# One input of two-input VectorE instructions moved from SBUF to PSUM in a four-block graph network

## What is computed

```
x = layernorm(x + L0(x))   # s, v = x @ w;  w0..w3 = silu(edge_attr_8 @ fc1) @ fc2 ;  tensor products of
                           # s[src], v[src] with edge_attr_4 and w0..w3;  segment_sum over dst;  @ w_lin2
x = layernorm(x + L1(x))   # four GCN layers (widths 128, 256, 256, 256 gathered), segment_sum over dst
x = layernorm(x + L2(x))   # mean of x[dst] over each src;  relu(x @ W_self.T + mean @ W_neigh.T + b)
x = layernorm(x + L3(x))   # attention of two heads: e = leaky_relu(a_src[src] + a_dst[dst]),
                           # alpha = segment_softmax(e, dst), segment_sum(xs[src] * alpha, dst), prelu
```

## Time and profile before

| | |
|---|---|
| median of 3 runs | 9904.8 us (9901.6 to 9915.3) |
| the profiled execution | 9888.5 us, span 9886.7 us |
| granted TensorE clock, mean | 0.777 |
| busy: POOL, PE, DVE, ACT | 6902, 5937, 5561, 2664 us |

### The profile page before, as it was taken

One profiled execution on the slowest core, in us unless ns is written; L12 is line 12 of the kernel. 1 busy time (PEld: TensorE's weight loads), 2 busy tenths in 40 slices (PEclk: granted clock), 3 DMA queues, 4 the chain that ended last, 5 costly groups with the idle time before them and its releaser, 6 DMA issues. The chain is left out here.

```text
span 9886.7 us, 100742 instructions
## 1 busy us (share of the span) xinstructions
PE 5937.4 (60%) x23034; PEld 4208.1 (43%) x23034; DVE 5560.9 (56%) x14363; ACT 2663.7 (27%) x8909; POOL 6902.3 (70%) x7265
## 2 busy tenths in 40 slices
PE   0676745555566665666656666555554444588785
PEld 0343433333444443444434444333343333476674
DVE  9307037777655556555565555544444333488887
ACT  0332335555322223111131111200001000366665
POOL 0678757777677765777657776577777777577775
PEclk9999986777788887888878888677765555577877
DMA  7111123333311122333323333233332111212112
GB/s 268 48 58 48 58 70 101 101 102 102 54 52 52 52 46 82 100 100 100 88 84 100 100 100 86 81 101 100 99 89 58 53 53 53 44 48 49 49 48 41
DMA packets 344415, 770.69 MB, mean 78 GB/s; under 512 B 121029, under 2 KB 175577, under 8 KB 337226
## 3 DMA queue, kind: packets, MB, share of 16 engines
q0 software_dynamic: 251328, 600.99, 23.1%
q1 hardware_dynamic: 85066, 105.97, 3.5%
q10 hardware_dynamic: 7488, 57.94, 1.5%
HBM read 616.04 MB, written 148.41 MB: 77 GB/s over the span
## 5 line engine op out<-in xcount | busy, mean ns | idle before, releaser
L566 DVE TENSOR_TENSOR acc<-acc,ps 128x256 f32 (+3 forms) x4992 | 1884.0, 377 | 2859.7 <-PE ps L903 2403.0
L903 PE MATMUL ps<-rows,hot 128*128 128x256 f32 (+2 forms) x5824 | 1645.2, 442 | 1712.3 <-issue 871.1
L741 POOL DMA_INDIRECT rows<-table_gcn,index_dst x2080 | 2082.6, 1001 | 684.9 <-issue 608.2
L903 PEld LDWEIGHTS ps<-rows,hot 128*128 128x128 f32 x5824 | 1281.7, 272 | 2152.3 <-issue 1145.9
L786 ACT ACTIVATE ut<-u,fld 128x128 f16<-128x128 f16 x1664 | 576.7, 393 | 2732.8 <-DVE u L829 2732.8
L497 POOL DMA_INDIRECT dst_rows<-pay,acc x782 | 798.7, 1021 | 529.5 <-ACT pay L481 304.6
L741 POOL DMA_INDIRECT rows<-table_gat,index_dst x832 | 913.1, 1097 | 262.6 <-issue 253.3
L741 POOL DMA_INDIRECT rows<-table_lin,index_dst x832 | 860.3, 1034 | 335.2 <-issue 241.4
L741 POOL DMA_INDIRECT rows<-table_mean,index_src x832 | 795.0, 955 | 259.0 <-issue 253.2
L718 PE MATMUL ps<-prod,hot 128*128 128x257 f32 x1664 | 637.4, 550 | 535.4 <-issue 347.5
L875 PE MATMUL ps<-prod,ut 128*128 128x416 f16 x3328 | 889.3, 399 | 0.0
(11 more groups left out here) (270 smaller groups left out, 9196.2 us busy)
## 6 DMA issues: line engine op xcount, KB each, us to landing
dst_rows<-pay ACTq DMA_DIRECT2D x52, 1088.0 KB, 31.6
fld<-dst_rows SPq DMA_DIRECT2D x104, 544.0 KB, 3.5
rows<-table_gcn,index_dst POOLq DMA_INDIRECT x2080, 2.5
table_gcn<-acc SPq DMA_DIRECT2D x15, 1024.0 KB
rows<-table_lin,index_dst POOLq DMA_INDIRECT x832
rows<-table_mean,index_src POOLq DMA_INDIRECT x832, 2.5
rows<-table_gat,index_dst POOLq DMA_INDIRECT x832
dst_rows<-pay,acc POOLq DMA_INDIRECT x782, 2.3
```

The costliest lines, as they stand in the source:

```text
L566: c.nc.vector.tensor_tensor(to, to, product, ALU.add).then_inc(c.added.sem, 1)
L741: pool.indirect_dma_start(to(q, j), None, table, bass.IndirectOffsetOnAxis(ap=c.idx[k][:, t:t + 1], axis=0)).then_inc(c.gathered[q % per]. ...
L903: pe.matmul(c.ps[:, j % ahead, 0:used], c.hot[:, r % 2, j, :], row_of(c, s, r, j, used), start=True, stop=True).then_inc(c.mm.sem, 1)
```

## The change

- In `sort_dve` the scan's operand of ones becomes one PSUM column, repeated.
- In all passes the one-hot's `c.iota` comes from a copy in PSUM (bank 3, in the attention bank 7), which ScalarE writes once a pass.
- In `messages` ScalarE writes the scaled vectors to PSUM banks 4 to 7, in one copy and not two; it waits for the same half of the group before. Products use three banks and not eight.
- In `aggregate` products use three banks, not four or eight.
- In `attend` ScalarE takes the exponential twice, first into PSUM (read by line 1969 as its second input), then into the weights' own columns (`m.kept`); products use two banks, not three.

Cut to its core:

```diff
@@ sort_dve
+    ones = c.ps[:, banks[1], 0:1]
+    st(dve.memset(ones, 1.0)).wait()
...
-            st(dve.tensor_tensor_scan(runs[i], s.one_row[:, :], masks[i], base[:, bass.ds(b * 2 + i, 1)],
+            st(dve.tensor_tensor_scan(runs[i], ones.broadcast_to([P, TC]), masks[i], base[:, bass.ds(b * 2 + i, 1)],
@@ helpers
+PLACES = 3
+def lay_places(c, act, bank=PLACES):
+    act.activation(c.ps[:, bank, 0:P], c.iota[:, :], ACT.Copy).then_inc(c.places_laid.sem, 1)
+def wait_places(c, dve):
+    dve.wait_ge(c.places_laid.sem, c.places_laid.n + 1)
 def one_hot(c, h, places):
-    c.nc.vector.tensor_tensor(c.hot[:, h, :, :], c.iota[:, :].unsqueeze(1).broadcast_to([P, G8, P]),
+    c.nc.vector.tensor_tensor(c.hot[:, h, :, :], c.ps[:, PLACES, 0:P].unsqueeze(1).broadcast_to([P, G8, P]),
@@ messages
+    ahead = 3
+    bank = lambda q, j: (q * G8 + j) % ahead
+    scaled_in = lambda b, t, j: c.ps[:, 4 + 2 * b:6 + 2 * b, (j % 4) * 3 * MUL:(j % 4 + 1) * 3 * MUL] if t is None else \
+        c.ps[:, 4 + 2 * b + t, 0:4 * 3 * MUL].rearrange("p (j a u) -> p j a u", j=4, a=3)
...
-                if not (first(i) and r < 2):
-                    act.wait_ge(m.prod.sem, q * 2 + (m.prod.n - 2))
                 for j in range(G8):
+                    if j % 4 == 0 and q:
+                        act.wait_ge(m.prod.sem, m.prod.n + q * 2 + j // 4 - 1)
...
-                        last = nc.scalar.activation(s.wev[:, r % 2, j, a, :, :], w13, ACT.Copy,
+                        to = scaled_in(j // 4, None, j)[:, :, a * MUL:(a + 1) * MUL]
+                        last = nc.scalar.activation(to, w13, ACT.Copy,
...
-                    nc.vector.tensor_tensor(s.dot, wev[:, :, :, 1, :], g[:, :, 1:4, :],
+                    nc.vector.tensor_tensor(s.dot, scaled_in(b, 1, 0), g[:, :, 1:4, :],
...
-                    nc.vector.tensor_tensor(s.prod4[:, js, 1:4, 0:MUL], wev[:, :, :, 0, :],
+                    nc.vector.tensor_tensor(s.prod4[:, js, 1:4, 0:MUL], scaled_in(b, 0, 0),
...
-                    if not (first(i) and r == 0):
-                        pe.wait_ge(c.added.sem, q * G8 + (c.added.n + j - G8 + 1))
-                    pe.matmul(c.ps[:, j, 0:AU], c.hot[:, r % 2, j, :],
+                    if q or j >= ahead:
+                        pe.wait_ge(c.added.sem, q * G8 + (c.added.n + j - ahead + 1))
+                    pe.matmul(c.ps[:, bank(q, j), 0:AU], c.hot[:, r % 2, j, :],
@@ aggregate
-    ahead = 4 if per or bins is not None else G8
+    ahead = 3
+    bank = lambda q, j: (q * G8 + j) % ahead
...
-                    add_chunk(c, dve, q, j, numbers[j], used, c.ps[:, j % ahead:j % ahead + 1, 0:used])
+                    add_chunk(c, dve, q, j, numbers[j], used, c.ps[:, bank(q, j):bank(q, j) + 1, 0:used])
@@ attend
+    places = 7
+    listed_in = lambda a, b: (6, 4, 0, 1)[2 * a + b]
+    weight8 = c.ps[:, 4, 64:64 + HEADS * G8].rearrange("p (j a) -> p j a", j=G8)
...
-                nc.scalar.activation(heads(s.wt)[:, :, :, CH], s.z[:, :, :], ACT.Exp).then_inc(m.powered.sem, 1)
+                nc.scalar.activation(weight8, s.z[:, :, :], ACT.Exp).then_inc(m.powered.sem, 1)
+                nc.scalar.activation(heads(s.wt)[:, :, :, CH], s.z[:, :, :], ACT.Exp).then_inc(m.kept.sem, 1)
...
-                nc.vector.tensor_tensor(hot_of(r), c.iota[:, :].unsqueeze(1).broadcast_to([P, G8, P]),
+                nc.vector.tensor_tensor(hot_of(r), c.ps[:, places, 0:P].unsqueeze(1).broadcast_to([P, G8, P]),
...
-                                        wt[:, :, :, CH:HW].broadcast_to([P, G8, HEADS, CH]),
+                                        weight8.unsqueeze(3).broadcast_to([P, G8, HEADS, CH]),
...
+                pe.wait_ge(m.kept.sem, q + (m.kept.n + 1))
                 for j in range(G8):
-                    before = j - 3 if j >= 3 else (-2, -1, -3)[j]
-                    if not (first(q) and before < 0):
-                        pe.wait_ge(c.added.sem, q * 2 * G8 + (c.added.n + 2 * before + 2))
-                    pe.matmul(c.ps[:, 5 + j % 3, 0:width], hot_of(r)[:, j, :], s.wt[:, j, :],
+                    if q or j >= 2:
+                        pe.wait_ge(c.added.sem, q * 2 * G8 + (c.added.n + 2 * (j - 2) + 2))
+                    pe.matmul(c.ps[:, 5 + j % 2, 0:width], hot_of(r)[:, j, :], s.wt[:, j, :],
```

More of the change, by code:

```diff
@@ L139, in __init__ @@
         self.added = sem("chunk_added")
+        self.places_laid = sem("places_laid")
     def sb(self, name, shape, dt=F32):
@@ L195, in _ @@
             st(dve.memset(s.lin2[:, :], 0.0))
-            st(dve.memset(s.one_row[:, :], 1.0))
             st(dve.memset(s.pos["dst"][:, :], 0.0))
@@ L572, in end_pass @@
     c.hot_ready.n += NG
+    c.places_laid.n += 1
     for g in c.gathered[0:per]:
@@ L625, in scaled @@
                         last.then_inc(m.scaled.sem, 1)
+            lay_places(c, nc.scalar)
             indices(0, 0)
@@ L691, in reduce @@
                 for j in range(4):
-                    add_chunk(c, dve, q, j, bins[j], AU, c.ps[:, j:j + 1, 0:AU])
+                    add_chunk(c, dve, q, j, bins[j], AU, c.ps[:, bank(q, j):bank(q, j) + 1, 0:AU])
                     products(i, r, 1, j + 1)
@@ L698, in reduce @@
                 for j in range(4, G8):
-                    add_chunk(c, dve, q, j, bins[j], AU, c.ps[:, j:j + 1, 0:AU])
+                    add_chunk(c, dve, q, j, bins[j], AU, c.ps[:, bank(q, j):bank(q, j) + 1, 0:AU])
                     if after(i, r, 1, RING):
                         products(*after(i, r, 1, RING), 0, j - 3)
+            wait_places(c, dve)
             hot(0, 0)
@@ L902, in product @@
                         pe.wait_ge(c.added.sem, q * G8 + (c.added.n + j - ahead + 1))
-                    pe.matmul(c.ps[:, j % ahead, 0:used], c.hot[:, r % 2, j, :], row_of(c, s, r, j, used),
+                    pe.matmul(c.ps[:, bank(q, j), 0:used], c.hot[:, r % 2, j, :], row_of(c, s, r, j, used),
                               start=True, stop=True).then_inc(c.mm.sem, 1)
@@ L1881, in body @@
                     factor(*nxt(i, r))
+            lay_places(c, nc.scalar, places)
             for a in range(HEADS):
@@ L1884, in _ @@
                     act.wait_ge(m.listed.sem, m.listed.n + 2)
-                    last = nc.scalar.activation(s.nt_of[:, b * half:(b + 1) * half, a], c.ps[:, (6, 7, 0, 1)[2 * a + b], 0:half],
+                    last = nc.scalar.activation(s.nt_of[:, b * half:(b + 1) * half, a], c.ps[:, listed_in(a, b), 0:half],
                                                 ACT.Copy)
@@ L1983, in add @@
                     nc.vector.scalar_tensor_tensor(to, to, s.factor[:, r % 2, j, a:a + 1],
-                                                   c.ps[:, 5 + j % 3, a * HW:(a + 1) * HW],
+                                                   c.ps[:, 5 + j % 2, a * HW:(a + 1) * HW],
                                                    ALU.mult, ALU.add).then_inc(c.added.sem, 1)
@@ L2082, in _ @@
                 for b in range(2):
-                    last = pe.matmul(c.ps[:, (6, 7, 0, 1)[2 * a + b], 0:half], s.scores_t[:, a * P:(a + 1) * P],
+                    last = pe.matmul(c.ps[:, listed_in(a, b), 0:half], s.scores_t[:, a * P:(a + 1) * P],
                                      s.bin_hot[:, b * half:(b + 1) * half], start=True, stop=True)
@@ L2100, in attend @@
         x.n += 4 * NG
-    for x in (m.looked, m.scored, m.powered, m.weighted, m.masked, m.maxed, m.factored):
+    for x in (m.looked, m.scored, m.powered, m.kept, m.weighted, m.masked, m.maxed, m.factored):
         x.n += NG
@@ L2169, in gnn @@
         s.pos = {k: lay(TC) for k in ("dst", "src")}
-        s.binf, s.mask, s.run, s.one_row = (lay(TC) for _ in range(4))
+        s.binf, s.mask, s.run = (lay(TC) for _ in range(3))
         s.ki = lay(TC, I32)
@@ L2199, in gnn @@
             "p (j a u) -> p j a u", j=4, a=3)
-        s.wev = s.hot_v[:, :, :, :].rearrange("p j a n -> p (j a n)").rearrange(
-            "p (h j a t u) -> p h j a t u", h=2, j=G8, a=3, t=2)
         s.ut = sb("ut", [P, 2, 4 * P])
```

1 line of the change is left out of this document (removed).

## The result

The changed kernel takes 9779.0 us (median of 4 runs, 9758.9 to 9785.2), the kernel before 9910.1 in the same series (4 runs): ratio 0.9863, 95% interval [0.9844, 0.9882]. It is faster, by 131 us. The forecast was 9670, with a range from 9610 to 9740: the gain came out about half as large, and the time lies above the range. The profiled execution has a span of 9780.6 us, 106 less than before's.

The account below looks back on a forecast made before the run. It took POOL's indirect DMAs to bound the passes, and a VectorE-ScalarE-VectorE loop the attention. Terms -35 - 197 - 61 + 57 = -236 us gave 9652 from the profile, 9670 for the runs' median; range 9610 to 9740.

Parts of the forecast that it names:

- the term of the attention: Attention: two banks make products wait for sums at the low clock; 57 us lost, bounds 0 and 134.
- the look-up is later: Attention, after the running maximum: VectorE loses another 0.6 us, but its 0.57 us wait for ScalarE leaves 0.1.
- Rival (2): Attention loses over 95 us, with chunks at the low clock: about 9735 us; chance 0.13.
- Scans: Second sort's second loop: scatters no longer held up by scans, 35 us gained, bounds 20 to 37.
- cost nothing: Scatter beside the second sort: freed scatters that fall into COPY_PREDICATED were said to lose no time.
- One-hots in GCN and mean: GCN and mean passes: gathers freed from one-hots, 197 us gained of 205 surplus, bounds 150 and 205.
- Tensor products: Tensor-product pass: one-hot and scaled-vector products get a PSUM input; 61 us gained, bounds 45 to 67.
- Rival (3): Tensor products become bound by VectorE, so 61 us stay: 9730 us; chance 0.08.
- PSUM as input and output: VectorE's reads from PSUM and ScalarE's writes to it: no change in time taken.
- rival (7): Tensor products: ScalarE's writes to PSUM cost double, 170 us more, 9840 us; chance 0.02.
- rival (5): Gathers are not freed by the PSUM inputs, the attention's loss stays: 9960 us, slower; chance 0.06.
- rival (4): The attention is coupled to POOL after all: another 126 us off, 9545 us; chance 0.03.

Follow-up runs that it names:

- e3: The changed kernel with each of the attention's eight one-hot transposes per group issued twice, two banks kept: 9653.0 us, ratio 0.9738 to the kernel before.
- e11: The kernel before (three banks in the attention) with each attention one-hot transpose issued twice: 9927.6 us, ratio 1.0023.
- e12: The kernel of e4 with each attention one-hot transpose issued twice: 9650.9 us, ratio 0.9743 to the kernel before.
- e7: The kernel before with only the scan's ones read from PSUM: 11511.7 us, ratio 0.9984, in a series where the kernel before took 11535.6 us.
- e9: The kernel before with only the five aggregate passes (four GCN, one mean) as in the change, in a repeat run: 9713.9 us, ratio 0.9809.
- e4: The changed kernel, but its attention keeps three banks and writes the first exponential to free columns of bank 4: 9624.6 us, ratio 0.9708 to the kernel before.
- e2: The kernel before with one edit, two banks in place of three for the attention's products: 10053.2 us, ratio 1.0143.
- e1: The changed kernel with the attention of the kernel before: 9634.2 us, ratio 0.9719 to the kernel before.

## Why the prediction was wrong

**The step that failed** is the term of the attention: "Sum 0.55 x 103 = 57 us lost". It measured +145 in the changed kernel, +150 with two banks alone. The wait itself was right: a product waits for the sum two before it, chiefly at the low clock. Its steps, as means over the groups, from before to after: first sum to `drop` 2.22 to 2.72 us (+0.50, forecast 0.45); `drop` to the last sum 1.97 to 2.56 (+0.59, forecast 0.6); scores to weighting 1.96 to 1.45 (-0.51: the slack of 0.57 absorbed it, as forecast). These come to 0.58 against 0.55. What the forecast disposed of with "the look-up is later" is last sum to next scores: 1.07 to 1.93, +0.86 us. The weighting to the first sum gave 0.06 back. Together 1.38 us, times 103 is 142.

Why it is so much shows when the groups are parted by their look-up. In 58 of 102 it runs at the high clock (1.87 us): a group takes 11.80 us, 0.47 over before, 48 us over 102 groups, close to the forecast. In 44 it runs mostly at the low clock (3.30 us), and a group takes 13.93: 44 x 2.13 = 94 us more. Before, none of the 102 was low. (The first group, low in both, is left out.) So the prediction took the granted clock as given, with the shares of the trace of before; but the edit itself changes it. A TensorE that waits between products of a group was granted less clock (0.78 to 0.67), with the low clock products take longer and wait again, and sixteen back-to-back matmuls, hidden before, come last. e3 shows that this, not the wait as such, is most of the loss: it keeps two banks, adds work, and gives back 123 of 145 us. e11 and e12 show the other half: with three banks the same added work costs 22 to 26 us. With the added transposes the stage takes 1295.0 us with two banks (e3) and 1296.1 or 1289.6 with three (e11, e12), so having one bank less costs next to nothing there.

Rival (2), over 95 us lost, is the one that came true. It was given 0.13. Its price, 9735, stands for a loss of some 123 us, and the term's upper bound was 134; 145 was measured, because both left the look-up's own length out. A range that held it would have needed the look-up's length at either clock, and both stand in the trace of before: 1.85 us, and 3.41 in the first group.

**Scans.** Right in size, -34 in the stage for 35, but with a wrong reading. In before, 51 scatters begin in a scan and lose 37.5 us together; after, 74 do and lose nothing. The freed ones fall in part into TENSOR_SCALAR, which has one tensor input (in SBUF) and holds them up too: 25 of them lose 0.32 us each, where 24 lost 0.16 before, 4 us more:

```profile
780.65 1.15 DVE L268 TENSOR_SCALAR acc<-acc,iota_b 128x782 f32<-128x782 f32 x2
780.81 1.27 POOL L499 DMA_INDIRECT dst_rows<-pay,acc  x1 [0.30 <-issue]
```

And COPY_PREDICATED doesn't "cost nothing". The scatter of the earlier trace rows begins within 0.02 us of the start of the second copy, and one that begins so early isn't held up by a one-hot either (five in before, 0.94 to 0.95 us; of those begun 0.04 to 0.1 us into a one-hot, 27 took 1.94 to 1.99). e7 has scatters that begin later in a copy, here with 0.7 us of it left, and they take 0.5 us too long:

```profile
942.93 2.17 DVE L276 COPY_PREDICATED acc<-acc 128x782 f32<-128x782 uint32 x2
943.24 1.48 POOL L499 DMA_INDIRECT dst_rows<-pay,acc  x1 [0.30 <-issue]
```

That the freed scatters of the changed kernel begin in the last 0.1 us of a copy, where they lose nothing, is luck. The row of the sum in the earlier trace rows, begun 0.03 us into it, was as weak a witness; there the conclusion holds, since 431 gathers of before begin well inside a sum of 256 columns in the GCN passes and take 946 ns on average.

**One-hots in GCN and mean.** -181 (e9: -185) for -197. The gathers' mean is 949 ns in the GCN passes; over 3328 gathers 3 ns above the undisturbed 946 are 10 us, where 8 were left in the sum. Line 847, a column instruction with one SBUF input, still costs some 195 gathers 55 ns each, which is all of it. The gathers themselves gave 196 us, as forecast. The other few us per pass lie in the ends of the passes.

**Tensor products.** -36 in the stage for -61, but the pass itself, first gather to last sum, went from 1138.0 to 1088.0. The gathers' surplus there fell from 73 to 22 us where 12 were left in the sum: 112 gathers in place of 91 begin in line 697 (679 before) and lose 19 us. The rest is the node work behind the pass, the same code in both, 14 us longer. Its windows in before, after and e12:

```profile
2551.00:2610.00 59.00, 36.38 (x294) 32.28 (x294) 44.66 (x224) 35.40 (x98) 27.63 (x105) 0.87 0.19 57
```

```profile
2467.00:2540.00 73.00, 59.22 (x294) 56.59 (x294) 44.32 (x223) 37.68 (x99) 27.65 (x106) 0.51 0.15 46
```

```profile
2470.00:2528.00 58.00, 36.24 (x294) 32.05 (x294) 43.98 (x223) 35.70 (x99) 27.70 (x105) 0.87 0.19 58
```

Granted clock 0.87 or 0.51. e12 and e4 differ only in the attention, long after, and have 58.6 and 72.8 us: so it is scatter, and no cost of the change; with one profile of each kernel, whether it goes by program or by execution stays open. The profile of before was a good one in both ways: e2, e9 and e11 have its code up to here and take 1213 to 1218 us for the stage, not 1196.6. Against those the change gives 52 to 57 us, close to the 61. These 17 to 21 us would account for most of why the profiles differ by 106 us and the runs by 131. Rival (3) is out: VectorE did not become the bound.

**PSUM as input and output.** Nothing, as taken: the one-hot takes 1218 ns from either; the weighting, line 1995, takes 1216 ns in the attention, where line 1969 took 1227. The fixed cost that the Trainium skill gives ("VectorE: DVE Perf Modes", TRN2 errata) isn't seen in these. ScalarE's 24 writes of scaled vectors take 5.78 us, as they took 5.82 in the earlier trace rows; rival (7) is out:

```profile
1600.57 5.78 ACT L640 ACTIVATE ps<-fld 128x64 f32<-128x64 f32 x24
```

**Freed gathers, rival (5).** Out: nothing over the undisturbed time in place of 512 ns. That also decides against the inference of the Trainium skill ("SBUF — State Buffer", "Who interferes with whom") that a `tensor_tensor` with two SBUF inputs leaves descriptor generation alone. Its rule that an instruction with at most one SBUF input leaves GpSimd alone holds outside what it calls the 2-port modes: the sums fit it, and TENSOR_SCALAR, which it names among the instructions that can enter such a mode, does hold up the scatters above. **Coupling of the attention to POOL, rival (4).** Out: two banks cost 150 us where its gathers are slow (e2, 840 us of POOL's time) and 145 where they are free (the changed kernel, 785), so 55 us of gathers were worth at most 5.

## What to carry to other kernels

Taking a buffer away between TensorE and a consumer is priced at TensorE's *future* clock, not at the clock of the profile in hand: look for every long burst of TensorE work that is hidden now, read its length at both clocks, and ask what waits for it. If such a stage is bound by waits of TensorE, work of no use between the waits can pay (here 126 us for 832 added transposes), but only where a burst at the low clock ends last; elsewhere it costs. To free POOL's indirect DMAs, give VectorE's long two-input instructions one input from PSUM wherever POOL sets the end, look at what the freed DMAs fall into next, and leave the stage alone where it doesn't: e1, which does only that, gives twice the gain of the whole change.

## What the runs showed of the hardware that was not expected

- One engine's waits lower TensorE's granted clock enough to double a later burst: look-ups of 1.85 us became 3.42, the mean clock of the stage 0.67 in place of 0.78, and 0.89 with eight instructions more a group.
- An indirect DMA that begins inside a one-hot or a scan with two SBUF inputs, a COPY_PREDICATED, or a TENSOR_SCALAR of 782 columns in SBUF loses what is left of it less 0.13 us (0.5 us with 0.7 us of a COPY_PREDICATED left, in e7). With a PSUM column in place of one of the scan's inputs it loses nothing (74 scatters). One that begins within 0.02 us of the instruction's start loses nothing either: five took 0.94 to 0.95 us in one-hots of before.
- The same node work, 294 matmuls, took 58.6, 63.5 or 72.6 us in the profiles of different kernels, at a granted clock of 0.87, 0.68 or 0.51.
- The same kernel took 9902 to 9912 us in some series and 11371 to 11536 in others, with gaps of several us on VectorE that nothing in the profile explains, and the record has a series of either kind on chip number 4. The order of two versions can turn around between them: the aggregates alone gave a ratio of 0.981 and of 1.008.
